# Flamingo block on one core: the value products of a quad in one block, behind the third score block and its maxima

## The reference

```python
def _L0_xattn_ref(x, y, Wq, bq, Wkv, bkv, q_gamma, q_beta, k_gamma, k_beta, Wproj, bproj):
    ...                                        # 16 heads of 8; y: 4 x 512 context tokens
    q = _layernorm(q, q_gamma, q_beta) * SCALE
    k = _layernorm(k, k_gamma, k_beta)
    attn = jax.nn.softmax(jnp.einsum('bhnd,bhmd->bhnm', q, k), axis=-1)
    out = jnp.einsum('bhnm,bhmd->bhnd', attn, v)
    ...
x = x + jnp.tanh(g_xattn[0]) * _L0_xattn_ref(_layernorm(x, axis=-1), ctx_1024, ...)
x = x + jnp.tanh(g_ffn[0]) * _L0_ffn_ref(...)     # routed experts of low rank
x = x + jnp.tanh(g_xattn[1]) * _L1_xattn_ref(...) # second attention, heads of 64
x = x + jnp.tanh(g_ffn[1]) * _L1_ffn_ref(...)     # routed experts
```

## Time and profile before

| | |
|---|---|
| median of 3 runs | 768.84 us (767.29 to 769.34) |
| profiled execution, span from first to last instruction | 768.1 us (the page gives no other time of it) |
| busy: PE, DVE, ACT, POOL | 717.8, 559.2, 359.7, 337.1 us |
| chain that ended last, by engine | PE 72%, DVE 21%, issue 4%, ACT 2% |
| first attention, q = 0 to 16 | from about 61 to about 195 us |
| granted TensorE clock, 60 to 300 us | 1.00 of full speed in each 20 us |

### The profile page before, as it was taken

How to read it: one execution, slowest core, us unless ns; L and a number is a source line. 1 busy time by engine, 2 the same in 40 slices (tenths; PEclk the granted TensorE clock), 3 DMA queues, 4 the chain that set the end, 5 groups by cost and what they waited for, 6 DMA issues and landing times.

```text
span 768.1 us, 14481 instructions
## 1 busy us (share of the span) xinstructions
PE 717.8 (93%) x5642; PEld 532.6 (69%) x5642; DVE 559.2 (73%) x1089; ACT 359.7 (47%) x531; POOL 337.1 (44%) x421
## 2 busy tenths in 40 slices
PE   6779999999998898999999999999999989999896
PEld 4656666666877776666776767767667756887895
DVE  4667887774798877887667866588966887587644
ACT  2657766666344345545544455355454445220300
POOL 3283534520443215666656666566665765100000
PEclk9879999999999999999999999999999999999999
DMA  8100000000600040000000000000000000000000
GB/s 180 18 1 2 3 1 2 1 3 1 220 1 0 1 109 2 1 2 1 2 1 1 2 1 2 1 2 1 2 2 1 1 2 1 1 8 1 8 8 7
DMA packets 25586, 11.58 MB, mean 15 GB/s; under 512 B 11856, under 2 KB 24224, under 8 KB 25392
## 3 DMA queue, kind: packets, MB, share of 16 engines
q1 hardware_dynamic: 24512, 10.60, 5.4%
q10 hardware_dynamic: 1008, 0.07, 0.1%
HBM read 10.08 MB, written 0.52 MB: 14 GB/s over the span
## 4 chain that ended last, share of the span: by engine, by line
PE 72%; DVE 21%; issue 4%; ACT 2%; DMA 1%; SPq 0%; DVEq 0%; ACTq 0%
PE ps L1736 69%; DVE o L1441 2%; PE ps L1747 2%; DVE mx L1111 2%; DVE pmax L1425 1%; DVE pmax L1428 1%; DVE kql L1416 1%; DVE exm L1307 1%; DVE ysum L1574 1%; DVE cn L1378 1%; ACT kqh L614 1%; DMA raw<-in_L_xattn_Wproj_dram 1%; PE ps L1840 1%; DVE rs_t L988 1%; DVE xnC L1222 1%
## 5 line engine op out<-in xcount | busy, mean ns | idle before, releaser
L854 ACT ACTIVATE p<-ps 128x1024 f32<-128x1024 f32 x96 | 96.3, 1026 | 123.4 <-PE ps L1736 123.3
L586 POOL TENSOR_TENSOR acc<-p 128x256 f32<-128x256 f32 x128 | 92.5, 755 | 91.2 <-ACT p L854 91.2
L1736 PE MATMUL ps<-p,v 128*64 128x256 f32 (+1 forms) x1280 | 130.2, 386 | 1.8 <-DVE o L1442 1.3
L592 POOL TENSOR_TENSOR acc<-acc,p 128x256 f32<-128x256 f32 x128 | 89.9, 733 | 54.7 <-ACT p L854 54.7
L1736 PE MATMUL ps<-kqh 64*128 64x256 f32 (+1 forms) x640 | 107.8, 365 | 5.6 <-DVE pmax L1425 3.1
L1425 DVE TENSOR_REDUCE pmax<-ps 128x2 f32<-128x1024 f32 x64 | 78.2, 1223 | 31.9 <-PE ps L1736 31.6
L1111 DVE TENSOR_REDUCE mx<-ps 128x1 bf16<-128x512 f32 x128 | 82.5, 687 | 26.0 <-PE ps L1736 25.4
L1736 PEld LDWEIGHTS ps<-p,v 128*64 128x64 f32 (+1 forms) x1280 | 63.3, 125 | 50.8 <-issue 18.8
L541 POOL TENSOR_SCALAR q<-qst,rmask 128x256 fp32r<-128x256 f32 x64 | 59.0, 939 | 58.8 <-ACT qst L614 58.8
L1736 PEld LDWEIGHTS ps<-kqh 64*128 64x128 f32 x640 | 61.4, 189 | 31.7 <-issue 21.7
L718 ACT ACTIVATE p<-ps 128x1024 f32<-128x1024 f32 x64 | 65.5, 1026 | 23.0 <-PE ps L1736 21.3
(11 more groups left out here) (294 smaller groups left out, 1603.0 us busy)
## 6 DMA issues: line engine op xcount, KB each, us to landing
w<-in_L_ffn_W_dram SPq DMA_DIRECT2D x1, 2048.0 KB, 12.1
wt<-in_L_ffn_W_dram SPq DMA_DIRECT2D x4, 512.0 KB, 6.1
ctx_all<-in_ctx_dram SPq DMA_DIRECT2D x4, 256.0 KB, 5.6
raw_kv<-in_L_xattn_Wkv_dram SPq DMA_DIRECT2D x1, 1024.0 KB, 5.0
raw<-in_L_ffn_B_dram SPq DMA_DIRECT2D x9, 64.0 KB
xr<-in_x_dram SPq DMA_DIRECT2D x4, 128.0 KB, 4.0
raw_q<-in_L_xattn_Wq_dram SPq DMA_DIRECT2D x1, 512.0 KB, 5.9
wout<-in_L_xattn_Wout_dram SPq DMA_DIRECT2D x1, 512.0 KB, 7.2
```

Of the source, the lines that this page charges most:

```text
L586: ins = pool.tensor_tensor(acc1[:, at], p1[:, s, 0, at], p1[:, s, 1, at], ALU.add)
L592: ins = pool.tensor_tensor(acc1[:, at], acc1[:, at], p1[:, s, 2, at], ALU.add)
L854: act.activation(p1[:, g % 2, u, :], bank(2 * (n % 2), 2), ACT.Exp, scale=SCALE1).then_inc(a_exp1.sem, 1)
L1736: return pe.matmul(o, lhsT, rhs, start=start, stop=stop)
```

## The change

In the branch for quads that are not turning, the call of `values0` between the second maxima pair and the third score block is taken out, and the call behind the third maxima pair issues all four key tiles in place of the last two. Nothing else is edited; the number of instructions and their operands stay the same.

```diff
                 else:
-                    if q >= 1:
-                        values0(q - 1, 0, TC // 2)
                     if q == AQ - 1:
                         common0(0, (1,))
                     scores0(4 * q + 2)
                     maxima(4)
                     if q == AQ - 2:
                         head0(0)
                     if q >= 1:
-                        values0(q - 1, TC // 2, TC)
+                        values0(q - 1)
                     scores0(4 * q + 3)
                     maxima(6)
                     if q == AQ - 1:
                         experts0(0)
                     if q >= 1:
                         outputs0(q - 1)
```

## The result

Twenty runs of the changed kernel have a median of 772.13 us (769.24 to 773.43), twenty of the kernel before 769.87 us. The ratio is 1.0029, with a 95% interval of 1.0015 to 1.0043: about 2.2 us slower, inside the forecast range and just under the 0.3% that the prediction took for a clear difference. One execution of the kernel before took 810.46 us and is not in the ratio. The profiled span grew from 768.1 to 770.4 us.

What follows compares the result with a forecast made beforehand. PE was taken as the bound, busy 93% of the span. Seven plain quads x 0.36 = 2.52, quads 6 and 11 0, q = 12 +0.20, q = 14 -0.22, q = 15 0: +2.5 us, so 771.3 us, range 769.3 to 773.4.

Steps and rivals of the forecast that it cites:

- the seven plain quads: Quads 1, 2, 3, 4, 7, 8 and 10 of the first attention: +0.36 us each, 2.52 in all.
- the tail: Quads 14 and 15, without maxima left: -0.22 us in quad 14, 0 in quad 15.
- The wait at the third maxima pair: At maxima(4), PE newly waits for DVE to reduce the second pair: 0.57 us, bounds zero to 0.70.
- The merge: One block of 32 value products replaces two of 16: -0.22 us per quad, 0.14 plus 0.07 to 0.08 for entering.
- T to the fourth score block: From the second maxima pair's start (T) to scores(4q+3) in plain quads: 4.05 us against 3.69.
- The weight loads: Ahead of the value block: if pulled ahead of running matmuls, 0.08 us would vanish per quad, about 0.6 in sum.
- Quads 6 and 11: Quads where DVE is the bound, 5.61 and 4.92 us between reductions, both above 4.69: the change costs 0.
- quad 12: Distance between DVE's reductions of maxima(2) and maxima(6) rises from 4.49 to 4.69 us: +0.20.
- Rival C: DVE's pauses no longer hide the change in quads 6 and 11: about +3.4 us, 772.2; chance 0.12.
- rival B: Part of the wait at maxima(4) is covered, quads cost 0.25 to 0.28: about +1.9 us, 770.7; chance 0.14.
- the wait for the gates' difference: In quad 15, common0 part 1 waits about 0.2 us for DVE's difference of the two best gates, eating the merge's 0.22.
- Rival A: At maxima(4) the reductions stay hidden and only the merge counts: -1.8 us, 767.1, not slower; chance 0.08.

Runs made afterwards that it cites:

- short reductions: Each DVE reduction of maxima cut to the first 128 of 512 columns: on the kernel before 758.03 us, on the changed kernel 756.45 us.
- experiment 3: Against the kernel before, all 32 value products between the second maxima pair and third score block, none behind the third pair: 774.59 us, ratio 1.0058.
- experiments 4 to 6: Changed kernel with value block halved around the fourth score block, 775.82 us; changed kernel with fourth score block directly behind the third, 766.94 us; and experiment 6.
- experiment 6: Kernel before with the value products merged behind the third score block only in quads 14 and 15: 768.00 us, ratio 0.9975.

## Why the prediction was right

The forecast was + 2.5 us, the stage shows + 2.45 and the timing + 2.2. The mechanism was right, and two of its terms were too small by the same amount, in opposite directions. That the total came so close is in part luck: the seven plain quads cost 2.66 us in place of 2.52, and the tail gave back 0.41 in place of 0.22. The chances leaned on the other side of the line, 0.52 for a clear slowdown; the timed 2.2 us lies just under the line of 2.3.

- *The wait at the third maxima pair* was put at 0.57 us and is 0.70. What failed is the step that built the time without a wait from 0.48 + 0.58 + 0.48. The 0.58 of a score block was read in the earlier trace rows behind a value block, and a score block pays there for leaving it; behind maxima it takes 0.48 (78.97 to 79.45 with short reductions). That is 0.10 of the 0.13; the rest is in the two terms of 0.48, which are about 0.46 there. The upper bound of 0.70, two single waits of 0.35, was the value. The end of the wait, 2.11 after T, was right, since both rows showed it.
- *The merge* was put at - 0.22 and is - 0.34: entering costs 0.10 (0.56 against 0.46), the block saves 0.14, and the same 0.10 of leaving was not counted. The ten waits for ACT that the kernel before lists are this leaving: they stand at scores behind value products, and there the weight loads idle for 0.41 us whichever releaser is named (90.28, "issue", in the changed kernel). The Trainium skill, "TensorEngine Tiling (Array Packing)", Tiling Modes, says that a change of tiling mode drains the engine. The trace agrees that the two changes saved cost time, 0.34 us; what the engine does in it, no row shows.
- Their sum, T to the fourth score block, was forecast as 4.05 and is 4.06. It was safe because it was taken from T to whole blocks, 2.11 + 0.08 + 1.86, and not from the two terms.
- *The weight loads* of the value block still start with its first product (88.42), after 0.24 us of idle loader. The rule of the Trainium skill, "TensorE: Matmul & The Clock Gate", Part 2, step 1, on weight loads pulled ahead doesn't show at this place, and the 0.6 us that it would have given did not come.
- *Quads 6 and 11* cost nothing (0.00 and - 0.02), and quad 12 costs 0.22 (0.20 forecast). Rival C falls with that, though its wait of 0.70 came true; rival B, plain quads at 0.25 to 0.28, falls with the 0.36 to 0.40 of the table.
- *The tail* gained 0.41 where 0.22 was forecast, by the same mis-sized merge. From the second score block to the fourth, quad 14 is shorter by 0.33 (forecast 0.22) and quad 15 by 0.09 (forecast 0). In quad 15 the wait for the gates' difference came as described, 0.20. PE's weight loads in the changed kernel:

```profile
185.24 0.73 PEld L1736 LDWEIGHTS ps<-xT,wt 128*128 128x128 f32 x4 [0.20 <-DVE wsel L1263]
```

- *Rival A* had the right sign for its case and the wrong condition. Made true by the short reductions, the order does gain, and by 3.6 us of stage rather than 1.8, since there all ten quads gain and the merge is worth 0.34.
- The median was worked out as span + 0.74. Over all runs of the changed kernel the time of an execution lies 1.7 to 2.2 us above its own span; the 0.74 set the median of three runs against the span of one execution, and so mixed this with the scatter between executions.

## What to carry to other kernels

Where one engine fills two buffers in turn and another empties them, the work standing between two fills must last as long as the emptying (here 1.3 us for two reductions); a filler may be moved only from a gap that has more than that. Merging two blocks of another array layout is worth its switch (0.34 us here), but only where the gap it leaves stays covered. A block's cost depends on what stands before it: take durations from a place with the same neighbours.

## What the runs showed of the hardware beyond what was expected

Executions differ by more than 2 us ahead of the stage. The six kernels with whole reductions run the same program up to the row turn of iteration 1, where the table starts; yet their profiled executions reach it at 68.79 (before), 68.68 (changed) and 68.53 us (experiment 3), or at 66.59, 66.35 and 66.40 (experiments 4 to 6). The chain that ended last, early in the kernel before:

```profile
12.51 7.70 PE ps L1736 x32
```

And the same 32 products in the kernel of experiment 6:

```profile
11.97 5.40 PE ps L1736 x32
```

They take 7.70 us in one execution and 5.40 in the other. That is as large as the effect under study. The timeline of PE tells which of them are slow; first the kernel before, with the four transposes ahead of the 32:

```profile
11.39 1.09 PE L1747 MATMUL ps<-ident,xn 128*128 128x128 f32 x4
12.51 3.75 PE L1736 MATMUL ps<-ctxT,wt 128*128 128x512 f32 x4
16.06 1.57 PE L1736 MATMUL ps<-xT,wt 128*128 128x256 f32 x4
17.47 2.75 PE L1736 MATMUL ps<-blk,sq 128*128 128x16 f32 x24
```

Then experiment 6:

```profile
10.85 0.63 PE L1747 MATMUL ps<-ident,xn 128*128 128x128 f32 x4
11.97 1.95 PE L1736 MATMUL ps<-ctxT,wt 128*128 128x512 f32 x4 [0.49 <-ACT ctxT L614]
13.76 1.03 PE L1736 MATMUL ps<-xT,wt 128*128 128x256 f32 x4
14.62 2.75 PE L1736 MATMUL ps<-blk,sq 128*128 128x16 f32 x24
```

The four products of 512 columns take about twice as long in the kernel before, and the 24 behind them the same 2.75 us. A factor of two is that between the clock's two levels, 1.2 and 2.4 GHz, and the pace fits it: the transposes of the kernel before start 0.21 us apart at 11.39, as its products of 128 columns do from 20.6 to 23.9 us, where the granted clock was 0.50, and 0.11 us apart in experiment 6. So the slow products most likely ran at the lower level. The profile doesn't show it directly, since it gives a granted clock of 1.00 for both stretches, and why the pace rose later in one execution was not tried. For differences of this size the length of the stage in one trace told more than five rounds of timing.
